# Final gated states turned on VectorE in 32x32 squares, and x1 added on GpSimd, in a four-layer graph kernel

## What is computed

```python
x = layernorm(x + attention(x, adj, q, k, v))               # x1
h = x                                                       # gated layer, 5 steps
for _ in range(5):
    m = adj @ h
    z = sigmoid(m @ w34 + h @ u3 + b);  r = sigmoid(m @ w4 + h @ u3 + b)
    h = (1 - z) * h + z * tanh(m @ w5 + (r * h) @ u5 + b)
x = layernorm(x + h)                                        # y1 = x1 + h, x2 = its norm
x = layernorm(x + sum_k(adj^k @ x @ weight_k))              # powers 0..3: y2, x3
f = relu(x @ psi + b);  msg = (adj * adj).T @ f
out = layernorm(x + relu([msg, x] @ phi1 + b) @ phi2 + b)   # y3, res
```

## Time and profile before

| | before |
|---|---|
| median of 3 runs | 1362.16 us (1362.12 to 1363.35) |
| the profiled execution | 1361.57 us |
| its span, from first to last instruction | 1359.8 us |
| mean granted TensorE clock | 0.994 of full speed |
| PE busy | 1328.3 us, 98% |
| DVE, ACT, POOL busy | 80%, 70%, 63% |

### The profile page before, as it was taken

The page is one execution under the profiler, slowest core; times in us unless marked ns, Lnnn a source line. Parts: engine busy times, 40 slices in busy tenths (PEclk is TensorE's granted clock), DMA queues, the critical chain, the costliest instruction groups (busy, mean ns, idle before and its releaser), DMA issues.

```text
span 1359.8 us, 27644 instructions
## 1 busy us (share of the span) xinstructions
PE 1328.3 (98%) x8638; PEld 1187.0 (87%) x8638; DVE 1084.3 (80%) x2546; ACT 956.1 (70%) x1727; POOL 862.6 (63%) x907
## 2 busy tenths in 40 slices
PE   8999989999999999999999999999899999999997
PEld 7999978888888888888888888887689999999996
DVE  4788878777778777787777887778688888888886
ACT  5788877777777777777777777776546666666664
POOL 5988886666666666666666666666335555555554
PEclk9999999999999999999999999999999999999999
DMA  3333332000020000120000110000212222222211
GB/s 107 93 96 106 97 116 63 1 0 0 23 86 17 0 0 0 39 85 0 0 0 0 55 40 1 0 0 17 70 55 71 71 69 69 69 69 69 69 39 40
DMA packets 60048, 61.25 MB, mean 45 GB/s; under 512 B 4690, under 2 KB 39380, under 8 KB 59988
## 3 DMA queue, kind: packets, MB, share of 16 engines
q1 hardware_dynamic: 59556, 60.31, 14.0%
q10 hardware_dynamic: 432, 0.20, 0.1%
HBM read 35.33 MB, written 25.17 MB: 44 GB/s over the span
## 4 chain that ended last, share of the span: by engine, by line
PE 91%; DVE 3%; ACT 2%; POOL 2%; issue 1%; DVEq 0%; POOLq 0%; ACTq 0%
PE psum L1111 6%; PE psum L752 5%; PE psum L754 5%; PE psum L731 5%; PE psum L379 3%; PE psum L1123 3%; PE psum L1125 3%; PE psum L795 3%; PE psum L784 3%; PE psum L797 3%; PE psum L796 3%; PE psum L767 3%; PE psum L786 3%; PE psum L789 3%; PE psum L772 3%; PE psum L771 3%
## 5 line engine op out<-in xcount | busy, mean ns | idle before, releaser
L706 POOL TENSOR_TENSOR rh_lo<-rh,rh_hi 128x512 fp32r<-128x512 f32 x160 | 206.8, 1293 | 250.9 <-ACT rh_hi L830 250.9
L712 POOL TENSOR_TENSOR h_lo<-h,h_hi 128x512 fp32r<-128x512 f32 x160 | 216.5, 1353 | 12.8
L830 ACT CAST rh_hi<-rh 128x512 fp32r<-128x512 f32 x160 | 99.4, 621 | 140.6 <-DVE rh L862 140.6
L843 DVE TENSOR_TENSOR psum<-psum,h 128x512 f32<-128x512 f32 x160 | 111.9, 700 | 102.9 <-ACT psum L834 102.9
L752 PE MATMUL psum<-adj_t_hi,hn_hi 128*128 128x256 f32 x640 | 164.2, 291 | 1.0 <-DVE m_lo L856 1.0
L754 PE MATMUL psum<-adj_t_hi,hn_lo 128*128 128x256 f32 x640 | 156.6, 280 | 0.0
L827 ACT ACTIVATE psum<-psum,bias_cols 128x512 f32<-128x512 f32 x160 | 106.6, 666 | 60.5 <-PE psum L772 58.7
L862 DVE TENSOR_TENSOR rh<-psum,h 128x512 f32<-128x512 f32 x160 | 110.1, 688 | 45.6 <-ACT psum L827 45.4
L752 PEld LDWEIGHTS psum<-adj_t_hi,hn_hi 128*128 128x128 f32 x640 | 121.0, 189 | 4.9 <-issue 1.8
L754 PEld LDWEIGHTS psum<-adj_t_hi,hn_lo 128*128 128x128 f32 x640 | 120.9, 189 | 3.0
L817 ACT ACTIVATE z<-psum,bias_cols 128x512 f32<-128x512 f32 x160 | 111.6, 698 | 0.0
(11 more groups left out here) (273 smaller groups left out, 4300.3 us busy)
## 6 DMA issues: line engine op xcount, KB each, us to landing
x_in<-in_x_dram SPq DMA_DIRECT2D x32, 256.0 KB, 3.0
x_dram<-x SPq DMA_DIRECT2D x32, 256.0 KB, 2.1
g_x<-x_dram SPq DMA_DIRECT2D x32, 256.0 KB, 3.3
h_dram<-h SPq DMA_DIRECT2D x32, 256.0 KB, 2.0
ht<-h_dram SPq DMA_DIRECT2D x32, 256.0 KB, 2.9
c_x<-x_dram SPq DMA_DIRECT2D x32, 256.0 KB, 3.0
out_dram<-res SPq DMA_DIRECT2D x32, 256.0 KB, 2.4
conv_in<-in_L_gnn_weight_dram SPq DMA_DIRECT2D x1, 448.0 KB, 5.2
```

The lines of the kernel that those rows point to most:

```text
L706: pool.tensor_tensor(rh_lo[:, q, :], rh[:, q, :], rh_hi[:, q, :].bitcast(F32), ALU.subtract).then_inc(rh_lo_done, 1)
L712: pool.tensor_tensor(h_lo[:, q, :], h[:, (g - 1) % G, :], h_hi[:, q, :].bitcast(F32), ALU.subtract).then_inc(h_lo_done, 1)
L843: dve.tensor_tensor(cb, cb, hg, ALU.subtract).then_inc(dif_done, 1)
```

## The change

- VectorE turns the final h of a group in 32x32 squares into a new buffer `squares` of two, in the slot after it was made, behind L843. It waits for h and for the store of the group two earlier. ScalarE's copy of the next set's h (L810) waits for the squares in place of the store.
- SyncE stores the squares with four DMAs of 32 partitions and 512-byte rows (64 KB each), so that DRAM holds h with nodes on partitions.
- In the convolution TensorE's turns of h (L1165) and VectorE's sum (L1457) go. GpSimd makes y1 = h + x1, read in runs of 32 elements; in slot s that of group s+1, behind x3t_lo and ahead of its wait for `var_done`. VectorE's moments wait for it.
- Tiles of x1 and h lie in the order block * 2 + batch from the attention on; the gated layer's products with the adjacency (L752, L754) write two pieces of a bank each. VectorE's gated loop is written out at the ends of sets, GpSimd's last convolution round too.

```diff
@@ attention: scalar and vector
+    def by_block(i):
+
+        return i % KC * GB + i // KC
...
-                    op = act.activation(x1[:, q, i, :], y[:, (u - LAG_NORM) % R, i, :], ACT.Identity,
+                    op = act.activation(x1[:, q, by_block(i), :], y[:, (u - LAG_NORM) % R, i, :], ACT.Identity,
@@ gated: sync
         def store(g, k):
-            sp.wait_ge(h_done, k * SET_SLOTS + (SET_SLOTS - G + g + 1))
-            sp.dma_start(h_dram[bass.ds(k * G + g, 1), :, :].rearrange("o p c -> (o p) c"), h[:, g, :])\
-              .then_inc(h_out[g], 16)
+            sp.wait_ge(squares_done, k * G + g + 1)
+            nodes = h_dram[bass.ds(k * G + g, 1), :, :].rearrange("o (q i) (a x) -> (o a) i q x", q=QUARTERS, a=QUARTERS)
+            for a in range(QUARTERS):
+                sp.dma_start(nodes[a, :, :, :],
+                             squares[32 * a:32 * a + 32, g % 2, :].rearrange("i (q x) -> i q x", q=QUARTERS))\
+                  .then_inc(h_out[g], 16)
@@ gated: tensor
                 for b in range(GB):
+                    dst = batch(psum[:, B_M, :], b)
                     for c in range(KC):
-                        i = b * KC + c
-                        pe.matmul(psum[:, B_M, b * N:(b + 1) * N], hn_hi[:, p, i, :], adj_hi[:, c, :],
-                                  start=(c == 0), stop=False)
...
+                        pe.matmul(dst, hn_hi[:, p, tile(b, c), :], adj_hi[:, c, :], start=(b == 0 and c == 0), stop=False,
+                                  skip_group_check=True)
...
@@ gated: scalar
-                        act.wait_ge(h_out[g], k * 16)
+                        act.wait_ge(squares_done, k * G + (g + 1 - G))
@@ gated: vector
+        def turn_squares(g, k):
+            dve.wait_ge(h_done, k * SET_SLOTS + (SET_SLOTS - G + g + 1))
+            if isinstance(k, int):
+                wait_count(dve, h_out[(g - 2) % G], 16 * QUARTERS * (k + (0 if g < 2 else 1)))
+            else:
+                dve.wait_ge(h_out[(g - 2) % G], k * (16 * QUARTERS) + (0 if g < 2 else 16 * QUARTERS))
+            dve.transpose(squares[:, g % 2, :].rearrange("p (q t j) -> p t q j", q=QUARTERS, t=TILES),
+                          h[:, g, :].rearrange("p (t q i) -> p t q i", q=QUARTERS, t=TILES)).then_inc(squares_done, 1)
...
                 dve.tensor_tensor(cb, cb, hg, ALU.subtract).then_inc(dif_done, 1)
+            if final is not None:
+                turn_squares((g - 5) % G, final)
@@ convolution: gpsimd
+        def residual(it, u):
+            s, q = it * U + u, u % 2
+            pool.wait_ge(y1_loaded[q], it * (32 * U // 2) + 32 * (u // 2 + 1))
+            wait_count(pool, x2_done, s - 1)
+            pool.tensor_tensor(y1[:, q, :, :].rearrange("p i (a j) -> p i a j", a=4),
+                               ht[:, q, :].rearrange("p (a i j) -> p i a j", a=4, i=TILES),
+                               x1[:, q, :, :].rearrange("p i (a j) -> p i a j", a=4), ALU.add).then_inc(y1_done, 1)
...
                 pool.tensor_tensor(x3t_lo[:, :], x3t[:, :], x3t_hi[:, :].bitcast(F32), ALU.subtract).then_inc(x3t_lo_done, 1)
+            if isinstance(it, int) and s == 0:
+                residual(0, 0)
+            if live(it, u, -1):
+                residual(it + (u + 1) // U, (u + 1) % U)
             pool.wait_ge(var_done, s + 1)
@@ convolution: tensor
-                pe.wait_ge(y1_loaded[u % 2], it * (32 * U // 2) + 32 * (u // 2 + 1))
-                wait_count(pe, y1_done, s)
-                for b in range(GB):
-                    for c in range(KC):
-                        mm = pe.transpose(psum[:, B_T1, cols(tile(b, c))], ht[:, u % 2, cols(b * KC + c)], ident[:, :])
-                mm.then_inc(y1_mm, 1)
@@ convolution: vector
-                dve.wait_ge(y1_mm, s + 1)
-                wait_count(dve, x2_done, s - 1)
-                dve.tensor_tensor(y1[:, u % 2, :, :].rearrange("p (c b) d -> p c b d", c=KC),
-                                  psum[:, B_T1, :].rearrange("p (c b d) -> p c b d", c=KC, b=GB),
-                                  x1[:, u % 2, :, :].rearrange("p (b c) d -> p c b d", b=GB),
-                                  ALU.add).then_inc(y1_done, 1)
                 dve.wait_ge(y1_done, s + 1)
```

More of the change, by code:

```diff
@@ L614, in gated_layer @@
     z = sb("z", [128, 2, COLS])
+    QUARTERS = 4
+    squares = sb("squares", [128, 2, COLS])
     B_HN, B_M, B_R, B_GATE, B_HN_ODD = 0, 1, 2, 4, 7
@@ L626, in gated_layer, with tile, batch @@
     rh_done, dif_done, inc_done, h_done = (sem(n) for n in ("rh_done", "dif_done", "inc_done", "h_done"))
+    squares_done = sem("squares_done")
+    def tile(b, c):
+        return c * GB + b
+    def batch(ap, b):
+        return ap.rearrange("p (c b n) -> p c b n", c=KC, b=GB)[:, :, b, :]
     def run(eng, slot, lags):
@@ L693, in sync @@
         for g in range(G):
-            sp.wait_ge(h_out[g], 16 * SETS)
+            sp.wait_ge(h_out[g], 16 * QUARTERS * SETS)
     def gpsimd(pool):
@@ L749, in slot @@
                 for b in range(GB):
+                    dst = batch(psum[:, B_M, :], b)
                     for c in range(KC):
-                        i = b * KC + c
-                        pe.matmul(psum[:, B_M, b * N:(b + 1) * N], hn_hi[:, p, i, :], adj_hi[:, c, :],
-                                  start=(c == 0), stop=False)
-                        mm = pe.matmul(psum[:, B_M, b * N:(b + 1) * N], hn_lo[:, p, i, :], adj_hi[:, c, :],
-                                       start=False, stop=(c == KC - 1))
+                        pe.matmul(dst, hn_hi[:, p, tile(b, c), :], adj_hi[:, c, :], start=(b == 0 and c == 0), stop=False,
+                                  skip_group_check=True)
+                        mm = pe.matmul(dst, hn_lo[:, p, tile(b, c), :], adj_hi[:, c, :], start=False, stop=(c == KC - 1),
+                                       skip_group_check=True)
                 mm.then_inc(m_mm, 1)
@@ L837, in vector, with slot @@
     def vector(dve):
-        def slot(base, g, k):
+        def turn_squares(g, k):
[6 more added lines that the diff above has]
+                          h[:, g, :].rearrange("p (t q i) -> p t q i", q=QUARTERS, t=TILES)).then_inc(squares_done, 1)
+        def slot(base, g, k, final=None):
             s = base + g
@@ L866, in slot @@
                 dve.tensor_tensor(hg, cb, hg, ALU.add).then_inc(h_done, 1)
-        yield from run(dve, slot, 4)
+        for g in range(G):
+            yield g
+            slot(0, g, 0)
+        for k in range(SETS):
+            base = k * SET_SLOTS
+            if k > 0:
+                for g in range(G):
+                    slot(base, g, k, final=(k - 1 if g < 5 else None))
+            with dve.Fori(base + G, base + SET_SLOTS - G, G) as step:
+                for g in range(G):
+                    slot(step, g, None)
+            if k < SETS - 1:
+                for g in range(G):
+                    slot(base + SET_SLOTS - G, g, None, final=(k if g >= 5 else None))
+        for s in range(SLOTS - G, SLOTS + 5):
+            slot(s // G * G, s % G, None, final=(SETS - 1 if s >= SLOTS - G + 5 else None))
+            yield s
     programs = {"sync": sync, "gpsimd": gpsimd, "tensor": tensor, "scalar": scalar, "vector": vector}
@@ L939, in graph_conv_layers @@
     res_out = [sem(f"res_out{i}") for i in range(2)]
-    y1_mm, x2t_mm, x3t_mm, f_mm, msg_mm, hid_mm, o_mm = (
-        sem("c_" + n) for n in ("y1_mm", "x2t_mm", "x3t_mm", "f_mm", "msg_mm", "hid_mm", "o_mm"))
+    x2t_mm, x3t_mm, f_mm, msg_mm, hid_mm, o_mm = (
+        sem("c_" + n) for n in ("x2t_mm", "x3t_mm", "f_mm", "msg_mm", "hid_mm", "o_mm"))
     w_mm = [sem(f"w_mm{j}") for j in range(2)]
@@ L966, in graph_conv_layers, with run @@
     res_half_done = sem("res_half_done")
-    def run(eng, slot, second=None):
+    def run(eng, slot, second=None, written_out=0):
         for s in range(PEELED * U):
@@ L975, in run @@
                 second(s // U, s % U)
-        with eng.Fori(PEELED, GROUPS // U) as it:
+        with eng.Fori(PEELED, GROUPS // U - written_out) as it:
             for u in range(U):
@@ L980, in run @@
                     second(it, u)
+        for s in range(GROUPS - written_out * U, GROUPS):
+            slot(s // U, s % U)
         for u in range(L_W):
@@ L1015, in slot @@
                 if isinstance(it, int) and s < U:
-                    sp.wait_ge(earlier["h_out"][s], 16)
+                    sp.wait_ge(earlier["h_out"][s], 64)
                 if isinstance(it, int) and s == U:
                     for done in earlier["h_out"]:
-                        sp.wait_ge(done, 16 * GROUPS // 8)
+                        sp.wait_ge(done, 64 * GROUPS // 8)
                 sp.dma_start(ht[:, u % 2, :], h_dram[bass.ds(s, 1), :, :].rearrange("o p c -> (o p) c"))\
@@ L1101, in drain @@
             last_power(LAST, ENTRY + 4)
-        yield from run(pool, slot)
+        yield from run(pool, slot, written_out=1)
         drain()
@@ L1154, in slot @@
                 mm.then_inc(f_mm, 1)
```

(10 more changed lines are left out.)

2 lines of the change are left out of this document (1 added, 1 removed).

## The result

The changed kernel takes 1477.2 us, median of 4 runs (1473.4 to 1482.3), against 1362.1 before: a ratio of 1.0845, 95% interval 1.0810 to 1.0881. The forecast was 1486, range 1448 to 1522. Numbers of lines are those of the kernel that the rows belong to; the GpSimd sum is L1096 in the changed kernel.

The account below looks back on a forecast made before the run. TensorE was full (98%), but an equally long chain beside it left next to nothing to gain. Profiled 1361.57 + 94 (ring with clock) + 5 (squares) + 25 (overlap) = 1485.6, forecast 1486 us, range 1448 to 1522.

Parts of the forecast that it names:

- The ring: Convolution: load, GpSimd sum, power, x2, x3t, features, res, next load wait in a circle; 14.34 us a slot, +74 us.
- The clock in the ring: Convolution: TensorE's idle stretches bring half clock once per slot, costing 0.8 us each; slots of 15.15 us.
- PEclk below 9: Sign expected in the profile's convolution stage: TensorE's granted clock reading under 9.
- Turns off TensorE: Convolution: removing 32 x 4 turns of h, 0.45 us a group, gains 0, at the very most 14 us.
- The chain that was read from one slot: Convolution: features, f_hi, res, c_hi, c_lo, second spread excludes the turns and ends 0.05 us before needed.
- Squares on VectorE: Gated layer: 32 squares of 0.6 us each; 4 us in set-start slots, 1 before sets; +5, from 1 to 15.
- 5.4 that I gave as a sign: Gated layer: slots that start a set were expected to go from 5.08 to about 5.4 us.
- The overlap: Where gated layer and convolution overlap: waits for sums and loads add 23 us, +25 with lower clock; 12 to 35.
- slot 1 would give 1.3 back: Overlap, convolution slot 1: its sum is ready, so it recovers 1.3 of slot 0's +3.8 us.
- the stretch of lower clock for which the prediction added 2: Overlap: lower TensorE clock behind each stall raises the sum from +23 to +25 us.
- The other two stalls: Overlap: waiting for group 2's load delays rh_lo by 9.6 us; group 3's load delays c_hi by 10.9.
- Four stores for one: SyncE: four issues take some 1.8 us; costs nothing in the gated layer, but counts at its end.

Follow-up runs that it names:

- experiments 1: Changed kernel, but from convolution slot 6 SyncE issues the next group's loads ahead of its wait for res, a slot earlier: 1384.2 us, ratio 1.0176.
- 2: Changed kernel with GpSimd's sum of the next group moved behind the shift of the slot, SyncE's order unchanged: 1381.0 us, ratio 1.0151.
- 4: Changed kernel with GpSimd's sum made twice, the first into a buffer nothing reads: 1526.5 us, ratio 1.1225.
- experiment 3: Changed kernel with 8 unused products on TensorE behind each group's outputs, ahead of its wait for x3: 1471.3 us, ratio 1.0808.
- experiment 7: The fifth experiment's kernel with four turns of a constant tile put back on TensorE, result unread: 1365.3 us, ratio 1.0016.
- fifth experiment: Changed kernel with loads a slot ahead, GpSimd's sums reordered, and the last set's h turned in the slot that makes it: 1362.7 us, ratio 1.0008.

## Why the prediction was right, point by point

- **The ring** (predicted 14.34 us a slot without the clock, measured 14.49 with the clock kept up, and 14.2 in its shortest slots). Cause and place are shown from both ends, by experiments 1 and 2, and that the sum is a member by 4. It began at group 7 and ended with group 31, 25 slots. From slot 6 to slot 31 the changed kernel is late by 1423.23 - 1046.45 - (1305.39 - 1019.89) = 91.3 us; predicted 94 (the two numbers of before are those of the same instructions).
- **The clock in the ring** (predicted 0.8 us a slot, measured 15.07 - 14.49 = 0.58). In the slot shown the lower level falls on the features, as worked out. But I had counted on it once in every slot, and the trace has it 14 times in the 25, so that the slots lie between 14.2 and 16.0. The 14.6 us that experiment 3 gave back are 1.0 for each: I had it too often and each too cheap, and that 0.8 comes near 0.58 was in part luck. The sign "PEclk below 9" showed in two of the 40 slices only.
- **Turns off TensorE: worth 0.** Right for the slots with res (0.04 by experiment 7 against 5, and 0.09 between 11.42 and 11.33). Not right outside: in slots 4 and 5, ahead of the first res, 10.91 us instead of 11.39, and in slot 31 another 0.55. In all 1.5 us that I had not counted. The chain that was read from one slot holds only where each of its members runs.
- **Squares on VectorE** (predicted +5, measured +2.0: VectorE's L872 in slot 154 starts 2.79 us later than L843 did before, of which 0.77 were there already in slot 12, ahead of all squares). The term was mis-sized twice: I had 4 us for the slots that start a set and 1 for those before it, and the runs show 0 and 2.0. VectorE's timeline at the start of a set:

```profile
571.00 0.70 DVE L872 TENSOR_TENSOR psum<-psum,h 128x512 f32<-128x512 f32 x1 [0.65 <-ACT psum L853]
571.61 0.70 DVE L864 STREAM_TRANSPOSE squares<-h 128x512 f32<-128x512 f32 x1
572.23 0.79 DVE L878 TENSOR_TENSOR hn_lo<-g_x,hn_hi 128x512 fp32r<-128x512 f32 x1
...
576.15 0.70 DVE L872 TENSOR_TENSOR psum<-psum,h 128x512 f32<-128x512 f32 x1 [0.72 <-ACT psum L853]
...
581.22 0.70 DVE L872 TENSOR_TENSOR psum<-psum,h 128x512 f32<-128x512 f32 x1 [0.65 <-ACT psum L853]
```

The square takes 0.70 us as its neighbours do. The slots are 5.15, then 5.07 us, no longer than before (5.08 in the earlier trace rows), and not the 5.4 that I gave as a sign. I had set a square of 0.6 us against 0.33 us of wait and counted the rest. But hn_lo, 1.01 us in the earlier trace rows, takes 0.79 now, so the rest is covered as well. Only the turn from one set to the next costs, 0.67 us a set.
- **The overlap** (predicted +25, measured 24.7: the first x3t is 27.5 us late, 2.0 of it squares and 0.8 from the attention). GpSimd's sum for VectorE's slot 0 came behind h_lo as worked out:

```profile
936.43 1.30 POOL L731 TENSOR_TENSOR h_lo<-h,h_hi 128x512 fp32r<-128x512 f32 x1
...
937.85 2.51 POOL L1096 TENSOR_TENSOR c_y<-ht,c_x 128x512 f32<-128x512 f32 x2
```

but VectorE's L872 behind it came 2.7 us later and not 3.8. That slot 1 would give 1.3 back was wrong; slots 156 to 160 lost another 2.2. Of these 1.2 lie in slot 157, behind the stall, where TensorE's granted clock was 0.50 from 942.0 to 948.4 us (1.00 in the same stretch before): there is the stretch of lower clock for which the prediction added 2. The other two stalls, with their releasers:

```profile
976.82 1.26 POOL L1096 TENSOR_TENSOR c_y<-ht,c_x 128x512 f32<-128x512 f32 x1 [12.33 <-DMA c_x<-x_dram]
...
979.29 1.26 POOL L725 TENSOR_TENSOR rh_lo<-rh,rh_hi 128x512 fp32r<-128x512 f32 x1
...
1010.05 1.26 POOL L1096 TENSOR_TENSOR c_y<-ht,c_x 128x512 f32<-128x512 f32 x1 [19.67 <-DMA c_x<-x_dram]
```

The rh_lo behind the load of group 2 started at 979.29, 17.1 us later than in the earlier trace rows; VectorE's slot 160 was 7.7 late already, so 9.4 were added (predicted 9.6). Behind the load of group 3 the c_hi followed x2:

```profile
1012.60 1.65 ACT L1416 ACTIVATE x<-c_y,c_shift,c_rstd 128x128 f32<-128x128 f32 x4 [12.74 <-POOL c_shift L1128]
1014.15 0.56 ACT L1363 CAST c_hi<-psum 128x512 fp32r<-128x512 f32 x1
```

1014.15 against 985.78 in the earlier trace rows, 28.4 us late, 11.3 more than VectorE's slot 163 ahead of it (predicted 10.9). The four parts are 2.7, 2.2, 9.4 and 11.3, in all 25.6, of which 0.9 is made good by the first x3t. So the two long stalls were right by themselves, while the total of 25 is met because an error of -1.1 and one of +3.5 happen to stand against the 2 for the clock: in part luck. The fifth experiment shows 21.5 to 22.9 us of it to be order and not work.
- **Four stores for one**: four issues took 1.77 us where 1.8 were taken.

The sum, 1485.6, is 6.7 us above the profiled execution of the changed kernel, 1478.9: 3 for the ring with its clock, 3 for the squares, 1.5 for the slots outside, less the 0.8 by which the attention ended later. The median is another 1.7 below; executions of this kernel lie up to 9 us apart.

## What to carry to other kernels

Before an operation is moved to an engine with idle time, ask what its operand's arrival hangs on: a wait for a load placed ahead of work which that very load is queued behind closes a ring, and the slot becomes the ring's length, here with TensorE busy for only 225 of 275 us. Issue such a load a slot earlier, or put the waiting operation last on its engine; the one was worth 93 us here, the other 96. And an engine busy 99% of the time doesn't mean that each microsecond taken off it is gained: look for the chain beside it which ends just in time (res was in it), and shorten that first; doing so brought half of what I had expected of it.

## What the runs showed of the hardware that I had not expected

- More products made the slot shorter: with 8 idle ones a slot the granted clock was 1.00 instead of 0.94, and the slot 0.58 us shorter than 15.07.
- A sum on GpSimd that reads its operand in runs of 32 elements 128 apart took 1.28 us, no more than GpSimd's difference of two contiguous operands of that size (1.29).
- VectorE's hn_lo with both operands in SBUF took 1.01 us in the kernel before and 0.79 to 0.81 behind a square that delayed it by some 0.2 us. What it shared with before wasn't tried.
- Runs of one kernel spread, and the spread goes with the granted clock: of the 12 runs of the fifth version the nine with a mean of 0.995 or more took 1359.5 to 1363.7 us, the three with 0.992 took 1366.0 to 1367.3. The 12 of the seventh run from 1359.9 us at 0.998 to 1368.1 at 0.992.
- The profiled executions of 5 and 7 show it in one place. They are 3.9 us apart the wrong way round, and their first x3t is at 1001.76 and 996.03. Of these 5.7 us, 2.3 are there in VectorE's slot 14 already; why the attention's end varies stays open. The rest comes between 970 and 1002 us, where the mean granted clock of the fifth is 0.89 and that of the seventh 1.00. The steady slots of versions 1, 2 and 5, which do the same work there in three profiles, agree to 0.01 us (11.33, 11.33, 11.34). So the slots, and not two single times, tell what the turns cost.
